# One gather column in 52 of the last pass copied row by row from SyncE

## What is computed

```python
def _L3_gnn_ref(x, edge_index, edge_weight, W1, b1, W2, b2):
    row, col = (edge_index[0], edge_index[1])
    msgs = edge_weight[:, None] * x[row]
    agg = jax.ops.segment_sum(msgs, col, num_segments=x.shape[0])
    h = (agg + x) @ W1.T + b1 + agg * x @ W2.T + b2
    out = jax.nn.leaky_relu(h, negative_slope=0.2)
    return out
...
h = jnp.maximum(_layernorm(x, axis=-1), 0.0)
x = x + _L3_gnn_ref(h, edge_index, edge_weight, L3_gnn_W1, L3_gnn_b1, L3_gnn_W2, L3_gnn_b2)
```

## Time and profile before

| | us |
|---|---|
| median of 3 runs | 11414.75 (11414.55 to 11419.16) |
| the profiled execution | 11416.3 |
| its span in the trace | 11414.6 |
| busy in the span: GpSimd, DVE, ACT, PE | 8183.3, 7216.1, 5414.5, 962.5 |

### The profile page before, as it was taken

The page is one execution under the profiler, slowest core; times in us unless marked ns, Lnnn a source line. Parts: engine busy times, 40 slices in busy tenths (PEclk is TensorE's granted clock), DMA queues, the critical chain, the costliest instruction groups (busy, mean ns, idle before and its releaser), DMA issues.

```text
span 11414.6 us, 38373 instructions
## 1 busy us (share of the span) xinstructions
PE 962.5 (8%) x3312; PEld 681.2 (6%) x3312; DVE 7216.1 (63%) x6971; ACT 5414.5 (47%) x6326; POOL 8183.3 (72%) x8632
## 2 busy tenths in 40 slices
PE   4122222221000000030000001000000000000001
PEld 3111111110000000010000001000000000000001
DVE  8845555553888888769999997445444443333334
ACT  6244444442666666557676765333333333333332
POOL 2177777777777777667777776777777767777776
PEclk8555665555555555565555555555555555555555
DMA  8756666663666666546666665333433333333333
GB/s 303 274 194 200 206 201 202 204 201 114 216 210 215 212 213 214 194 153 221 224 222 223 224 221 159 96 113 110 113 110 113 111 94 106 103 106 104 105 106 103
DMA packets 793613, 1946.22 MB, mean 171 GB/s; under 512 B 214049, under 2 KB 425977, under 8 KB 792952
## 3 DMA queue, kind: packets, MB, share of 16 engines
q1 hardware_dynamic: 461360, 1129.25, 28.0%
q0 software_dynamic: 331904, 814.65, 25.4%
q10 hardware_dynamic: 144, 0.41, 0.0%
HBM read 1204.91 MB, written 738.73 MB: 170 GB/s over the span
## 4 chain that ended last, share of the span: by engine, by line
POOL 60%; issue 23%; DVE 9%; DMA 4%; ACT 2%; PE 1%; POOLq 0%; DVEq 0%; SPq 0%; ACTq 0%
POOL region L1374 57%; DMA region<-x,ix_s 2%; DVE psR L1505 2%; POOL work L1800 1%; DVE region L654 1%; DVE region L655 1%; DVE psB L1422 1%; DVE work L1520 1%; ACT work L1614 1%; DVE psR L1513 1%; DMA region<-h,ix_s 1%; POOL start_rows_by_dst L1132 0%; POOL start_ed L969 0%; PE psR L757 0%; POOL start_rows_by_src L1127 0%
## 5 line engine op out<-in xcount | busy, mean ns | idle before, releaser
L1520 DVE TENSOR_TENSOR_SCAN work<-work,psR 128x1792 f32<-128x1792 f32 (+2 forms) x496 | 1971.4, 3975 | 92.5 <-DVE ix_s L1441 56.5
L1374 POOL DMA_INDIRECT region<-x,ix_s x1612 | 1520.8, 943 | 502.6 <-issue 458.7
L1374 POOL DMA_INDIRECT region<-qm,ix_s x1612 | 1524.0, 945 | 492.6 <-issue 490.4
L1374 POOL DMA_INDIRECT region<-kv,ix_s x1612 | 1523.9, 945 | 491.1 <-issue 480.4
L1374 POOL DMA_INDIRECT region<-h,ix_s x1612 | 1521.0, 944 | 491.3 <-issue 487.0
L1374 POOL DMA_INDIRECT region<-k,ix_s x1612 | 1520.9, 943 | 491.3 <-issue 491.0
L1538 ACT COPY work<-region 128x1664 f32<-128x1664 f32 (+1 forms) x496 | 1162.4, 2344 | 1297.2 <-DMA region<-start_rows_by_dst 763.3
L1422 DVE TENSOR_TENSOR_SCAN psB<-psB,work 128x1792 f32<-128x1792 f32 (+1 forms) x496 | 1485.1, 2994 | 399.0 <-ACT psB L1551 353.7
L1614 ACT COPY work<-work 128x1664 f32<-128x1664 f32 (+2 forms) x496 | 1539.0, 3103 | 0.0
L1613 ACT COPY psR<-work 128x128 f32<-128x128 f32 (+2 forms) x496 | 189.4, 382 | 2464.3 <-DVEq L1521 2464.3
L1450 DVE TENSOR_TENSOR work<-region,psB 128x1664 f32<-128x1664 f32 x372 | 702.4, 1888 | 807.6 <-DMA region<-k,ix_s 527.4
(11 more groups left out here) (336 smaller groups left out, 5055.3 us busy)
## 6 DMA issues: line engine op xcount, KB each, us to landing
region<-start_rows_by_dst SPq DMA_DIRECT2D x248, 832.0 KB, 6.8
state_p<-work SPq DMA_DIRECT2D x124, 936.0 KB, 4.9
state_p<-work SPq DMA_DIRECT2D x124, 884.0 KB, 3.8
region<-start_rows_by_src SPq DMA_DIRECT2D x124, 832.0 KB, 7.4
start_rows_by_dst<-zero_t SPq DMA_DIRECT2D x62, 1664.0 KB, 7.6
state_pA<-work SPq DMA_DIRECT2D x124, 832.0 KB, 4.9
state_p<-work SPq DMA_DIRECT2D x124, 832.0 KB, 3.5
start_rows_by_src<-zero_t SPq DMA_DIRECT2D x1, 59904.0 KB, 163.6
```

The costliest lines, as they stand in the source:

```text
L1374: g_.indirect_dma_start(rows_s[b][:, k, 0:wd_s], None, q.tabs, bass.IndirectOffsetOnAxis(ap=ix_s[b][:, k:k + 1], axis=0))\
L1520: c.do(nc.vector.tensor_tensor_scan(q.st[:, 0:F * (K + 1)], decay_at(q, b)[:, 0:F * (K + 1)], summed[:, 0:F * (K + 1)], 0.0, ALU.mult, ALU ...
```

## The change

In P3 the halves are taken in 31 groups of four, 52 columns. In every group but the first, the last column of the fourth half is no longer gathered by GpSimd. Its 128 rows are copied by SyncE, one DMA per row, from `x3_t` into an HBM tensor `rows_ahead`, during the group before. When the buffer is free, SyncE moves them with one DMA into the column of `rows_s[1]`, and DVE waits for that too (`ahead_in`).

To address a row, SyncE needs its number in a register. `numbers_dve`, `numbers_pe`, `numbers_act` and `numbers_sp` turn every 52nd column of `oth_i[1]` into a row of 128 numbers and store it to HBM (the first three ahead of pass PA, the last after P1). In P3 SyncE loads 32 numbers with one instruction (`rows_ahead_sp`), with a check of each against its bounds, and issues 32 row copies ahead of each half's store. The semaphores that count gathers are now shared between passes (`Pass.rows`), with a base added.

```diff
+        numbers_f = sb("numbers_f", [P, IT // 4])
+        numbers_i = sb("numbers_i", [IT // 4, P], I32)
...
+        numbers_t = dram("numbers_ahead", [IT // 4, P], I32)
+        ahead_t = dram("rows_ahead", [IT // 4, P, 264])
...
+            def rows(self, b, value):
+
+                i = passes.index(self)
+                return S(f"rows{b}_{i % 3}"), value + (i // 3) * 16 * K * (IT // 2)
...
+            q.ahead = q is P3
...
-            with g_.Fori(0, IT // 2) as i:
+
+            def pair(i, short):
                 for b in range(2):
                     g_.wait_ge(*q.on(f"free{b}", i + 1))
                     if q is P1:
                         g_.wait_ge(q.own(f"next{b}"), i + 1)
                     g_.sem_inc(S("pool_go"), 1)
-                    for k in range(K):
+                    for k in range(K - (short and b)):
                         g_.indirect_dma_start(rows_s[b][:, k, 0:wd_s], None, q.tabs, bass.IndirectOffsetOnAxis(ap=ix_s[b][:, k:k + 1], axis=0))\
-                          .then_inc(q.own(f"rows{b}"), 16)
+                          .then_inc(q.rows(b, 0)[0], 16)
+
+            if q.ahead:
+                pair(0, False)
+                pair(1, False)
+                with g_.Fori(1, IT // 4) as j:
+                    pair(j * 2, False)
+                    pair(j * 2 + 1, True)
+            else:
+                with g_.Fori(0, IT // 2) as i:
+                    pair(i, False)
+
+        def gathered(q, i, b):
+
+            return 16 * (K * (i + 1) - (b * ((i + 1) // 2 - 1) if q.ahead and i > 0 else 0))
 
...
-                v.wait_ge(q.own(f"rows{b}"), i * (16 * K) + 16 * K)
+                v.wait_ge(*q.rows(b, gathered(q, i, b)))
+                if q.ahead and b and i % 2 and i > 1:
+                    v.wait_ge(S("ahead_in"), 16 * (i // 2))
...
+        LAST = 4 * K - 1
+        PART = P // 4
+
+        def numbers_dve(v):
+            line(v).do(nc.vector.tensor_copy(numbers_f[:, :], oth_i[1][:, LAST:T:4 * K]))
+            v.sem_inc(S("numbers"), 1)
+            v.wait_ge(S("numbers"), 3)
+
+        def numbers_pe(pe):
+            pe.wait_ge(S("numbers"), 1)
+            nc.tensor.transpose(psA[0:IT // 4, 0:P], numbers_f[:, :], ident[:, :]).then_inc(S("numbers"), 1)
+
+        def numbers_act(act):
+            act.wait_ge(S("numbers"), 2)
+            nc.scalar.copy(numbers_i[:, :], psA[0:IT // 4, 0:P]).then_inc(S("numbers"), 1)
+
+        def numbers_sp(sp):
+            sp.wait_ge(S("numbers"), 3)
+            sp.dma_start(numbers_t, numbers_i[:, :]).then_inc(S("numbers"), 16)
+            sp.wait_ge(S("numbers"), 19)
+
+        def rows_ahead_sp(sp, q, j, part):
+
+            a = part * PART
+            numbers = nc.values_load_multi_w_load_instructions(numbers_t[j:j + 1, a:a + PART],
+                                                               engines=(mybir.EngineType.SP,), min_val=0, max_val=PADN)[1]
+            for r in range(PART):
+                sp.dma_start(ahead_t[j, a + r:a + r + 1, 0:q.tabs.shape[1]], q.tabs[bass.ds(numbers[r], 1), :]).then_inc(S("rows_ahead"), 16)
+
+        def ahead_in_sp(sp, q, j):
+
+            sp.wait_ge(S("rows_ahead"), j * (16 * P))
+            sp.wait_ge(*q.on("free1", j * 2 + 2))
+            wd = q.tabs.shape[1]
+            sp.dma_start(rows_s[1][:, K - 1, 0:wd], ahead_t[j, :, 0:wd]).then_inc(S("ahead_in"), 16)
+
+        def pass_ahead_sp(sp, q):
+            for b in range(2):
+                sp.sem_inc(q.s(f"sent{b}"), 16)
+            for nm in q.needs:
+                sp.wait_ge(S(nm[0]), nm[1])
+
+            def four(j, first, last):
+                for part in range(4):
+                    if part == 2 and not first:
+                        ahead_in_sp(sp, q, j)
+                    if not last:
+                        rows_ahead_sp(sp, q, j + 1, part)
+                    pass_store(sp, q, j * 2 + part // 2, part % 2)
+
+            four(0, True, False)
+            for j in range(1, IT // 4 - 1):
+                four(j, False, False)
+            four(IT // 4 - 1, False, True)
...
+            numbers_sp(sp)
             proj_sp(sp, "j2", [(h2_t, 0, D + 4), (ed2_t, D + 4, D + 8)])
             pass_sp(sp, P2)
             proj_sp(sp, "j3", [(x3_t, 0, D)])
-            pass_sp(sp, P3)
+            pass_ahead_sp(sp, P3)
...
             v.sem_inc(S("edges_ready"), 1)
+            numbers_dve(v)
             pass_dve(v, PA)
...
+            numbers_act(act)
             pass_act(act, PA)
...
+            numbers_pe(pe)
             carry_pe(pe, PA)
```

## The result

| | before | changed |
|---|---|---|
| median, us | 11414.65 (11414.49 to 11419.16, 4 runs) | 13547.9 (13545.05 to 13550.97, 4 runs) |
| span of the profiled execution, us | 11414.6 | 13545.0 |
| last pass, first gather to last store, us | 2023 | about 4154 |

The ratio is 1.1869 (95% interval 1.1855 to 1.1883): 2133 us slower. The forecast was 12,240 us with a range of 11,370 to 12,900, and the measured time lies above it. The side and the mechanism were right, and the size was too small by a factor of 2.6. The ratios further down are against runs of the kernel before from the same session as each experiment, with medians of 11,414 to 11,418 us.

A forecast was written before the change was run, and what follows sets the result against it. GpSimd's gathers bound the last pass; SyncE, at 23.5 us per half against 15.91, would take over: 120 x 23.5 + 26 = 2846 us against 2023, +824 with the numbers' 1.5, on 11414.75: 12,240 us, range 11,370 to 12,900.

The forecast's parts named there:

- What bounds it, and who waits for whom: Last pass: GpSimd's gathers set the pace before; after, SyncE's work per half does, through waits of ACT, DVE and GpSimd.
- The gain: Last pass, GpSimd: 30 gathers fewer at 1.248 us take 37.4 us off the path if their replacement keeps up.
- The terms of SyncE's sum: SyncE's new work per half of the last pass, 23.5 us against the 15.91 available, in 120 halves.
- 32 DMA issues: SyncE, per half: 32 row copies at 0.47 us each, 15.0 us (9.3 to 20.5).
- address and `MOVE`: SyncE, per half: one register instruction per row for its address, at 0.07 us, 2.2 us.
- 32 checks, two instructions each: SyncE, per half: 64 register instructions that bound the numbers, at 0.07 us each, 4.5 us.
- load of 32 numbers: SyncE, per half: one load from HBM as one round trip, 1.24 us; up to 32 times that if per number.
- store, column load: SyncE, per half: the half's store and a quarter of `ahead_in`, 0.48 us.
- rival 4: Last pass: row packets make DMA engines the bound; at twice the packet price about 12,100 us; chance within a 0.55 case.
- the one that was left out with 0.12: SyncE, last pass: load or register instructions dominate, 47 or 62 us per half, 15,000 to 16,900 us; above 12,900, chance 0.12.
- Rival 1, it hides: Last pass: SyncE's work stays under 15.91 us per half, a row under 0.44 us; 11,379 us, chance 0.28.
- The numbers ahead of PA: Before pass PA: DVE waits for its copy, PE's transpose and ACT's copy, 1.5 us on the path.

The follow-up runs named there:

- loads_only: Changed kernel with the loads of numbers and checks kept, row copies left out, column filled from a fixed block: 11,377.6 us, ratio 0.9966.
- fixed_sbuf: fixed_rows, but each row goes as one piece into one partition of an SBUF tile, which fills the column: 11,382.0 us, ratio 0.9968.
- act_share: Changed kernel with rows into SBUF as one piece each, no checks, and 8 of each 32 rows issued by ACT: 11,377.9 us, ratio 0.9967.
- fixed_16: fixed_rows, but each row goes as 16 pieces into 16 SBUF partitions, column filled from a fixed block: 11,396.6 us, ratio 0.9984.
- eight_nc: Changed kernel with one column in 104, 16 rows per half, and no checks: 11,400.2 us, ratio 0.9984.
- fixed_rows: Changed kernel with row numbers written into the program: no load, no checks, no address in a register: 12,012.1 us, ratio 1.0523.

## Why the prediction was wrong, step by step

**What bounds it, and who waits for whom.** Right. SyncE took over the pace. The wait that was named, ACT for the landing of the store, is there with 2412.4 us. One on the same queue was missed: the load of the column stands behind the row copies too, and DVE waits 1782.5 us for it. It changes nothing in the pace.

**The gain.** Right: 37.4 us off the path where the rest is hidden (`loads_only`, `fixed_sbuf`, `act_share`: 36 to 39 us less).

**The terms of SyncE's sum.** This is the step that failed; the other factors of the formula held. Per half:

| term | predicted, us | measured, us | why |
|---|---|---|---|
| 32 DMA issues | 15.0 | 17.3 | 0.54 with its gap for 0.47 |
| address and `MOVE` | 2.2 | 4.7 | a second instruction, and a gap around each |
| 32 checks, two instructions each | 4.5 | 8.2 | 0.257 per number for 0.14 |
| load of 32 numbers | 1.24 | 3.5 | 0.1 for each number |
| store, column load | 0.5 | 0.7 | |
| sum | 23.5 | 34.4 | |

All five were too small, and 11 us in 120 halves are the 1310 us that the forecast lacks. The largest miss was the checks. Their price was in the trace of before and I didn't ask for it: I took 0.07 us from a handover, where the view of the flag's source line has the same instructions, on the same queue:

```profile
L585 SPq TENSOR_LOAD <-flag_i x4: 278/362/466, 496.2 to 4834.6; - x4
L585 SPq FUSED_REGOPS  x4: 154/158/194, 496.7 to 4834.9; - x4
L585 SPq SEQ_ASSERT  x4: 18/18/33, 497.0 to 4835.1; - x4
```

0.158 + 0.018 and two gaps are 0.26 per number, 8.2 us per half. With it alone the forecast is 27.2 us per half and 12,680 us. The load was a misreading of another kind: the same rows split my 1.24 us into 0.36 for the load and the rest, but only one number was loaded, so that the slope could not be seen. I took the lower bound of it although the upper was 32 times as high; the Trainium skill's price ("Runtime: NRT & Kernel Launch", section "Instruction fetch mechanics"), an estimated 6.4 us, which I set aside, would have erred on the other side by 2.9 us. For the DMA issues I wrote that the pieces are as few as in the cheap ones, though the order shows 16 x 8 and my rival 4 counts 16 pieces; the cheap ones went from one partition, and one piece against 16 made 0.17 us in `fixed_16`. The forecast's range took one high price at a time (0.64 per DMA) and never all prices a little above the middle, which is what came: 34.4 is inside no case but the one that was left out with 0.12.

**Rival 1, it hides.** Its condition, under 0.44 us per row with everything in it, was right, and the changed kernel is at 0.94 (0.686 + 0.257). Every run whose sum on SyncE comes under GpSimd's pace is faster: `loads_only`, `fixed_sbuf`, `act_share` and `eight_nc`.

**Rival 4, the DMA engines.** Out. It priced a piece of 32 bytes like a gather's packet. In the changed kernel's last pass (packets, MB, share of 16 engines)

```profile
q1 hardware_dynamic: 144768, 108.13, 7.9%
```

eight times the packets of before take 7.9% of 4144 us, 0.036 us each, stores included. `fixed_rows` moves as many pieces in 1536 us less.

**The numbers ahead of PA.** About right. DVE waits 1.26 us for ACT's copy:

```profile
2796.45 1.55 DVE L1435 MEMSET work<- 128x1792 f32 x1 [1.26 <-ACT numbers_i L1695]
```

and the first gather of PA has 2.93 us of idle time ahead of it, where it had 1.88: 1.05 us for the 1.5 predicted.

## What to carry to other kernels

When work is moved to an idle queue, ask how much time per period it has there, and price every instruction that the move issues in it, the register instructions, bounds checks and register loads too. The view of one source line has them where timeline and waits don't; if one such instruction ran anywhere in the trace of before, its price is there. Where many prices are bounded on one side only, they err together: let the range hold the case that each is a little dearer. And the shape and destination of a small DMA can matter more to the issuer than where its address comes from: rows into one partition of SBUF, no bounds checks and a share for a second queue, all three together, turned 19% slower into 0.3% faster.

## What the runs showed of the hardware

- A DMA's issue on SyncE by shape, 512 bytes each, fixed address: one piece into SBUF 0.25 us, 16 pieces into SBUF 0.42, 16 pieces from HBM to HBM 0.59. With the address in a register: 0.23 for one piece, 0.49 for the 16 to HBM, and two register instructions of 37 and 29 ns ahead of it.
- Loading registers took 0.36 us for one number, 1.15 for 8 (on ACT), 1.83 for 16, 2.9 for 24 and 3.5 to 3.9 for 32, from SBUF (3.4) as from HBM (3.5) in the changed kernel's setting.
- A bounds check of a register took two instructions, 147 and 18 ns, and 0.257 us with the gaps.
- 3840 row copies did not make GpSimd's own instructions longer: its gathers took 943 ns before and after.
- With fixed addresses, one or two of the first DMA issues behind a store took 0.5 to 1.4 us in place of 0.25 to 0.59.
